# Second cross-attention of a two-layer decoder: the division one half batch later on VectorE, the query matmuls ahead of the turnings on TensorE

## The reference

```python
xn, ln = layer_norm(x, ...), layer_norm(latents, ...)
q = (ln @ Wq).reshape(b, m, 8, 64)
k_x, v_x = split(xn @ Wkv); k_l, v_l = split(ln @ Wkv)
k_x = rope_rotate_k(k_x)
k, v = concatenate([k_x, k_l]), concatenate([v_x, v_l])
attn = softmax(einsum('bhid,bhjd->bhij', q * 64 ** -0.5, k))
out = einsum('bhij,bhjd->bhid', attn, v) @ Wo
```

## Time and profile before

| | us |
|---|---|
| median of 3 runs (1686.15 to 1689.84) | 1686.38 |
| the profiled execution's time | 1688.66 |
| its span | 1686.9 |
| TensorE busy (share of the span) | 1440.7 (85%) |
| VectorE busy | 879.0 (52%) |
| ScalarE busy | 600.6 (36%) |
| GpSimd busy | 583.3 (35%) |

### The profile page before, as it was taken

The page is one execution under the profiler, slowest core; times in us unless marked ns, Lnnn a source line. Parts: engine busy times, 40 slices in busy tenths (PEclk is TensorE's granted clock), DMA queues, the critical chain, the costliest instruction groups (busy, mean ns, idle before and its releaser), DMA issues.

```text
span 1686.9 us, 29468 instructions
## 1 busy us (share of the span) xinstructions
PE 1440.7 (85%) x10056; PEld 1117.0 (66%) x10056; DVE 879.0 (52%) x2481; ACT 600.6 (36%) x1481; POOL 583.3 (35%) x547
## 2 busy tenths in 40 slices
PE   7767998847999999997899996887776766999987
PEld 3554676526999999973466664655555544999976
DVE  7353565461212232129898514566666842676656
ACT  4203544321212212224334324443434212666652
POOL 2002012412222232216523320023434463776765
PEclk9898999968999999999999997998897887999999
DMA  7771000119889888822100105042433699655528
GB/s 224 189 253 51 2 14 27 64 50 368 325 313 339 301 316 322 307 72 97 63 1 1 38 1 167 26 141 94 152 109 114 247 308 321 176 174 172 168 69 339
DMA packets 137154, 274.67 MB, mean 163 GB/s; under 512 B 14378, under 2 KB 105672, under 8 KB 130736
## 3 DMA queue, kind: packets, MB, share of 16 engines
q1 hardware_dynamic: 112576, 218.23, 38.8%
q0 software_dynamic: 17520, 39.88, 6.6%
q10 hardware_dynamic: 6912, 14.68, 2.4%
HBM read 205.05 MB, written 61.11 MB: 158 GB/s over the span
## 4 chain that ended last, share of the span: by engine, by line
PE 45%; issue 13%; POOL 8%; DMA 5%; DVE 4%; SPq 2%; ACT 1%; POOLq 1%; ACTq 0%; DVEq 0%
PE bank L158 42%; POOL xe L1850 5%; DMA arena<-in_banka 2%; DMA arena<-yr 2%; PE bank L2382 2%; DVE arena L1625 1%; POOL yr L2523 1%; SPq L2589 1%; PE bank L1194 1%; SPq L2560 1%; POOLq L171 1%; POOL arena L196 1%; DMA arena<-xd,arena 1%; POOL arena L1558 0%; SPq L2561 0%
## 5 line engine op out<-in xcount | busy, mean ns | idle before, releaser
L158 PE MATMUL bank<-arena 128*128 128x128 f32 (+10 forms) x8728 | 1298.7, 341 | 174.4 <-ACT arena L2061 46.0
L158 PEld LDWEIGHTS bank<-arena 128*128 128x128 f32 (+5 forms) x8728 | 976.2, 184 | 453.3 <-issue 262.5
L2523 POOL DMA_INDIRECT yr<-arena x159 | 171.3, 1077 | 92.5 <-ACT arena L2453 53.6
L1239 DVE TENSOR_SCALAR arena<-bank,arena 128x128 f32<-128x128 f32 x188 | 52.9, 344 | 271.2 <-PE bank L158 271.2
L196 POOL TENSOR_TENSOR arena<-arena 128x1 f32<-128x1 f32 (+1 forms) x48 | 38.0, 792 | 363.7 <-DVE arena L188 363.6
L1274 POOL DMA_INDIRECT arena<-xd,arena x47 | 46.1, 981 | 250.8 <-PE bank L1194 215.6
L1850 POOL DMA_INDIRECT xe<-arena x112 | 112.0, 1000 | 32.8 <-issue 32.5
L2488 DVE COPY arena<-arena 128x768 f32 x127 | 76.6, 603 | 57.6 <-issue 57.4
L2055 ACT ACTIVATE arena<-bank,arena 128x256 f32<-128x256 f32 x128 | 59.0, 472 | 101.9 <-DVE arena L2127 101.9
L1217 ACT ACTIVATE arena<-bank 128x256 f32<-128x256 f32 x47 | 18.1, 384 | 211.4 <-PE bank L158 211.4
L1226 ACT ACTIVATE arena<-bank,arena 128x128 f32<-128x128 f32 x188 | 53.7, 368 | 91.8 <-PE bank L158 91.8
(11 more groups left out here) (264 smaller groups left out, 1470.7 us busy)
## 6 DMA issues: line engine op xcount, KB each, us to landing
arena<-in_bank SPq DMA_DIRECT2D x47, 2052.0 KB
arena<-xe SPq DMA_DIRECT2D x159, 129.0 KB, 2.4
arena<-kd SPq DMA_DIRECT2D x16, 1024.0 KB, 10.9
arena<-arena SPq DMA_DIRECT2D x16, 896.0 KB, 7.2
arena<-in_bank SPq DMA_DIRECT2D x8, 1536.0 KB, 10.9
arena<-yr SPq DMA_DIRECT2D x16, 768.0 KB, 15.5
kxv<-arena ACTq DMA_DIRECT2D x16, 512.0 KB, 2.6
arena<-kxv SPq DMA_DIRECT2D x16, 512.0 KB, 4.0
```

The source lines that it names most:

```text
L158: return t.matmul(o, l, r, start=start, stop=stop, skip_group_check=True)
L1239: h = v.tensor_scalar(h_ring[i % 3][:, (4 + m) * 128:(5 + m) * 128], banks[b][:, m * 128:(m + 1) * 128], sbc(w_ring[i % 5], 4100 + m), 0.0 ...
L2523: p.indirect_dma_start(yr, bass.IndirectOffsetOnAxis(ap=sidx.bitcast(I32)[:, n:n + 1], axis=0), y2_ring[n % NY], None, bounds_check=14335, ...
```

## The change

Two edits in `steps_f`, both in the loop over `i`.
- `dv` was yielded for half `i` late in step `i`. Now it is yielded for half `i - 1` right behind `sc` of step `i`. `f_m`, which holds minimum, sum and reciprocal, has four places and `f_s` two, as before.
- The preparation of the next group (`before[s]`) stood behind `tr` and `kv1`. Now it stands ahead of `ow`, `tr` and `kv1`.

```diff
                 else:
                     yield "z5", 6
                     yield "z6", 6
+                if 0 <= i - 1 < 32:
+                    yield "dv", i - 1
+                if g + 1 < 4:
+                    for u in before[s]:
+                        yield u, g + 1
                 if odd and 0 <= nb - 1 < 16:
                     yield "ow", nb - 1
                     yield "norm", nb - 1
...
                     yield "tr", i - 1
                 if odd and nb + 1 < 16:
                     yield "kv1", nb + 1
-                if g + 1 < 4:
-                    for u in before[s]:
-                        yield u, g + 1
-                if i < 32:
-                    yield "dv", i
                 if not odd and 0 <= nb - 1 < 16:
                     yield "pv", nb - 1
```

## The result

| us | before | after |
|---|---|---|
| median of 4 runs each | 1686.27 (1685.77 to 1689.84) | 1708.53 (1704.32 to 1709.07) |
| ratio to before, 95% interval | | 1.0111 [1.0095, 1.0128] |
| profiled execution: time, span | 1688.66, 1686.9 | 1709.07, 1707.3 |
| from the first scores to the shared expert's first matmul | 291.3 | 310.2 |

A forecast was written before the change was run, and what follows sets the result against it. No engine is full; a ring of waits through TensorE, VectorE and ScalarE, with VectorE's backlog, bounds the stage. Group sums gave -3.5 us, clock falls +3, so -0.5: 1685.9 at the median, forecast 1686, range 1677.5 to 1694.

The forecast's parts named there:

- The ring and VectorE's backlog: Second cross-attention: scores, minimum, exponential, copy, values wait in turn; VectorE's 4.3 us routing tail delays minimum 18, causing the 6.92 us wait.
- What the change removes: VectorE's idle time before L2133 goes; key copies in halves 12 to 15 and 20 to 23 no longer wait behind turnings.
- What it adds: Turning i-1 waits for minimum i and division i-1, 2.9 us after scores i; even halves wait 0.7 more for copies.
- TensorE's clock: Falls to 1.2 GHz after stalls in the stage: two of eight new stalls fall, +3 us, bringing -3.5 to -0.5.
- the eight new stalls: Stalls of 2.25 to 2.9 us in halves 8, 14, 16, 22, 24, 27, 28, 31, between harmless 2.56 and dear 3.12.
- The sum beneath it: Hand-set instruction order of the stage's halves, by groups: +2.2 +0.5 -0.4 -3.5 -0.9 -2.7 +1.3 = -3.5 us.
- my -3.5: Net of the hand-ordered groups over the stage, in us, before the +3 us for clock falls.
- The start: Halves 0 to 3: turning 0 comes at 8.2 us instead of 6.8; group 27.8 against 25.6, a loss of 2.2.
- The second: Slower rival: TensorE falls to 1.2 GHz after the eight insufficiently covered turnings; 1691 to 1696, taken as 1693; chance 0.20.
- The third: Rival that nothing moves: GpSimd's scatters behind its root at 1328.25 set the end; 1686.4, chance 0.05.
- The signs: In the stage: L1924's wait for L2137 grows from 7.2 to 20 to 30 us, L2061 and L2043's falls to about 10.
- the conditions for "wrong": L1924's waits under 15 us, groups 16 to 19 and 24 to 31 changing over 3 us, or clock moving over 0.05.

The follow-up runs named there:

- The later routing: Kernel before with the one-hot routing piece z6 moved from the second half of each four to the third: 0.9869, repeated 0.9910; stage 277.6 and 277.4 us.
- second pair of executions: Unedited changed kernel and unedited kernel before, each rerun on another chip: ratios 1.0113 and 1.0000 to the kernel before, stages 315.3 and 295.1 us.
- Fills in the kernel before: Kernel before with 3 to 7 extra useless float32 matmuls ahead of the values' wait in ten halves: ratio 0.9921, stage 286.4 us.
- the fills with turnings: Changed kernel with 24 or 48 extra 128x128 turnings ahead of the turning's wait in eight halves: ratio 1.0100 to the kernel before, stage 311.2 us.
- the control: Kernel before, nothing edited, traced on a chip of the experiments' set: ratio 1.0000, stage 295.1 us.
- the kernel edited in the covered halves alone: Both edits only in halves 12 to 15 and 20 to 23, old order elsewhere, against the kernel before: 1.0025 and 1.0059.

## Why the prediction was wrong

- **The ring and VectorE's backlog: right.** The later routing shortened the stage by 17.7 us with the same instructions.
- **What the change removes: right in the waits, smaller in the gain.** L2133 waits no longer, and the key copies wait 7.2 us where they waited 38.7. The covered groups gained 2.5 and 1.7 us, forecast as 3.5 and 2.7, and 0.6 and 0.9 in the second pair of executions.
- **What it adds: right.** The waits before the turnings of halves 16 to 19 were forecast as 2.9, 0.95, 6.4 and 1.6 us and came as 2.91, 0.87, 6.01 and 1.61.
- **TensorE's clock: the step that failed.** The prediction said of the eight new stalls: "I take two of the eight to fall, +3 us." The clock fell in halves 8, 16, 24 and 28 of these, and again in 10, 18, 26 and 30. It fell as the wait ended, so the turning ran slow too (1.93 for 1.09 us, and in half 16 then 6.78 for 4.98). A stall of 2.9 us is paid at 2.6 us (0.8 and 1.8 in half 16), not 1.6. I had placed 2.9 us between one harmless 2.56 and one dear 3.12, and leaned on the harmless one. Halves 14 and 22 fell behind 2.07 and 2.08 us in one execution and not behind 2.08 in another, and with the division's edit alone the turning of half 15 took 1.92 us after 2.01. So no figure in between was safe. The reading of the earlier trace rows beneath it was loose as well: the groups 12 to 15 and 20 to 23, set against those with long waits, had waits of 4.2 us and falls in halves 14 and 22 themselves.
- **The sum beneath it was built on the same assumption.** Its group lengths are those of a held clock but for one slow stretch in halves 10, 18, 26 and 30. By groups the forecast was 27.8, 36.4, 37.2, 39.5, 37.2, 39.5, 36.0 and 34.2 us; measured were 30.6, 36.7, 41.6, 40.5, 41.4, 40.5, 40.3 and 38.7. The four uncovered groups are 4.2 to 4.5 us above it, while their idle time came as written down (13.25 and 13.75 us in 16 to 19). The order itself never was a gain. TensorE's idle time rose by 11.7 us, and my -3.5 came out only because the sum gave the change the slow stretches of the kernel before as regained. By the estimate above those cost 26.5 us before (half of 53.0), and they cost 30.7 now. Fills in the kernel before regain them without the change (-8.7 us).
- **The start: mis-sized.** The group 0 to 3 was forecast 2.2 us longer and is 5.0 longer, at a clock of 0.73.
- **The rivals.** The second named the right mechanism, a fall in the new stalls. Of its eight places four fell (six in the second execution). It was too small (up to 1696), since it priced a fall without the slow turning and added it to a sum that already counted a held clock elsewhere. The third, that the end absorbs the shift, is excluded by the root at 1351.20 and the span, 20.4 us longer. The rule of the Trainium skill ("TensorE: Matmul & The Clock Gate", "Part 4: PE-mode transpose"), that turnings don't count as a busy array, has the fills with turnings against it: 24 turnings in the stall of half 8, then the real turning in 1.09 and the 56 matmuls in 4.98 us.
- **The signs.** L1924's wait for L2137 was to be 20 to 30 us and is 56.1. I had not summed my own hand order, whose 16 to 19 alone has 11.85. The one for L2061 and L2043 was to fall to about 10 and is 18.4 (16.7 and 1.7). Of the conditions for "wrong", the one on the groups 16 to 19 and 24 to 31 came true, and so did the one on the clock: it moved from 0.86 to 0.79 in 8 to 11 and from 0.92 to 1.00 in 12 to 15.

## What to carry to other kernels

A wait moved from one engine's instruction to another's is priced by what stands beside it there: the same two edits lose where nothing follows the scores, and where 3.6 us of independent matmuls do they range from a gain of 2.5 us in four halves (12 to 15) to a loss of 0.8 (4 to 7, which had no backlog to gain from). When a sum of the new order assumes the full clock, work the old order out at the full clock too; else the change is credited with what it doesn't bring. And where VectorE delivers a short reduction that a whole ring waits for, look first for long work that is queued ahead of it: moving one piece of some 3.4 us back by a half gave about 1%, where no reordering of the ring gained anything.

## What was not expected of the hardware

- Where the changed kernel has a stall of 2.9 us, TensorE fell to 1.2 GHz at its end or within the turning behind it. Stalls of 2.07 us, a turning and 1.05 us more led to a fall in one execution and not in another. In the trace of before a wait of 2.56 us had been harmless.
- Turnings held the 2.4 GHz level as matmuls did (4.98 us for the 56 matmuls behind either).
- The kernel before takes 1686 us on one chip and 1748 to 1759 on others. In the stage only 3.8 us of this lie (291.3 and 295.1), and single pieces are as long (4.98 and 1.09 us on both). Behind the stage ScalarE waits 20.4 and 27.5 us before entries 1299 and 1301 of its list in the control, with no releaser, where the first chip's trace has 14.7 and 5.6 us for TensorE.
- ScalarE's waits with no releaser in the trace stand at the same numbered entries of its list in kernels with different orders (1054 and 1154 in the control, 1052 and 1053 or 1152 and 1153 in the kernel edited in the covered halves alone). What causes them stays unexplained.
